# A residual block's second convolution in two goes of 32 output channels, on eight 64x32 tiles of TensorE, with half of the last pass behind the second go

## What is computed

```
x = x + _L0_conv_ref(_gn(x), w1, b1, gamma1, beta1, w2, b2, gamma2, beta2)
...
identity = x
out = conv3x3(x, quantize_weight(w1, W_BITS), b1)
out = jax.nn.relu(batchnorm(out, gamma1, beta1))
out = conv3x3(out, quantize_weight(w2, W_BITS), b2)
out = batchnorm(out, gamma2, beta2)
out = jax.nn.relu(out + identity)
```

## Time and profile before

| | |
|---|---|
| median of 3 runs | 535.56 us (535.4 to 535.96) |
| time of the profiled execution | 536.91 us |
| its span, first to last instruction | 535.1 us |
| busy share of the span | PE 73%, DVE 86%, ACT 62%, POOL 16% |
| first convolution | 14 to 206 us |
| second convolution | 212 to 402 us |
| last pass | 402 to 535 us |

### The profile page before, as it was taken

The page is one execution under the profiler, slowest core; times in us unless marked ns, Lnnn a source line. Parts: engine busy times, 40 slices in busy tenths (PEclk is TensorE's granted clock), DMA queues, the critical chain, the costliest instruction groups (busy, mean ns, idle before and its releaser), DMA issues.

```text
span 535.1 us, 20532 instructions
## 1 busy us (share of the span) xinstructions
PE 392.8 (73%) x9501; PEld 351.2 (66%) x9501; DVE 462.4 (86%) x593; ACT 331.4 (62%) x350; POOL 83.3 (16%) x147
## 2 busy tenths in 40 slices
PE   3999999999999999999999999999991000000000
PEld 1899889999999787899888998888880000000000
DVE  7999989999999757988988887798877999798995
ACT  3898799999999955765555566655515923544200
POOL 2027226666551500000000000000000000000000
PEclk9999999999999999999999999999996555555555
DMA  8934874433333000143333300000066999999997
GB/s 267 358 129 132 269 265 159 181 129 131 129 135 129 8 8 6 46 171 152 129 127 128 124 2 4 4 3 4 2 244 208 355 429 381 431 429 428 432 429 318
DMA packets 21965, 99.21 MB, mean 185 GB/s; under 512 B 6520, under 2 KB 8952, under 8 KB 16504
## 3 DMA queue, kind: packets, MB, share of 16 engines
q1 hardware_dynamic: 20256, 81.55, 40.4%
q10 hardware_dynamic: 1624, 16.36, 7.2%
HBM read 61.48 MB, written 35.50 MB: 181 GB/s over the span
## 4 chain that ended last, share of the span: by engine, by line
PE 72%; DMA 14%; DVE 10%; issue 2%; ACT 1%; SPq 0%; DVEq 0%
PE conv_ps L994 70%; DMA xa<-in_x_dram 11%; DVE slots L948 4%; DVE slots L951 3%; DMA out_dram<-xa 2%; DMA slots<-in_x_dram 1%; DVE xa L951 1%; DVE conv_ps L948 1%; PE conv_ps L957 1%; ACT split L435 0%; DVE gn_tup L674 0%; PE wt_ps L994 0%; PE stat_ps L994 0%; PE conv_ps L992 0%; DVE bn_tup L775 0%
## 5 line engine op out<-in xcount | busy, mean ns | idle before, releaser
L994 PE MATMUL conv_ps<-split,wmat 64*64 64x385 f16 (+3 forms) x9144 | 377.7, 324 | 2.1 <-ACT split L435 1.4
L994 PEld LDWEIGHTS conv_ps<-split,wmat 64*64 64x64 bf16 x9144 | 339.1, 107 | 37.6 <-issue 2.3
L469 ACT ACTIVATE slots<-conv_ps,par,evac_scale 128x784 f32<-128x784 f32 x124 | 123.7, 998 | 95.3 <-PE conv_ps L994 93.4
L775 DVE BATCH_NORM_STATS2 bn_tup<-slots 128x6 f32<-128x392 f32 x166 | 81.9, 555 | 15.6 <-ACT slots L469 15.6
L600 ACT ACTIVATE slots<-slots,skip_b,bn_w 128x3136 f32<-128x3136 f32 (+3 forms) x20 | 45.8, 2340 | 47.6 <-DVE slots L951 29.9
L674 DVE BATCH_NORM_STATS2 gn_tup<-slots 128x6 f32<-128x448 f32 x112 | 61.8, 612 | 0.9 <-DMA slots<-in_x_dram 0.9
L742 DVE TENSOR_TENSOR split<-slots,split 128x3136 f16<-128x3136 f32 (+4 forms) x36 | 57.2, 1607 | 3.5 <-ACT slots L449 0.9
L744 DVE SCALAR_TENSOR_TENSOR split<-slots,split 128x3248 f16<-128x3248 f32 (+3 forms) x18 | 53.6, 2979 | 2.3
L728 DVE TENSOR_SCALAR slots<-slots,bn_w 128x3248 f32<-128x3248 f32 (+3 forms) x18 | 30.4, 1688 | 21.4 <-ACT split L427 20.9
L427 ACT ACTIVATE split<-slots,bn_w 128x3248 f16<-128x3248 f32 x14 | 43.2, 3083 | 0.0
L477 ACT ACTIVATE xa<-conv_ps,par,evac_scale 128x784 bf16<-128x784 f32 x40 | 39.7, 994 | 0.0
(11 more groups left out here) (124 smaller groups left out, 214.4 us busy)
## 6 DMA issues: line engine op xcount, KB each, us to landing
out_dram<-slots SPq DMA_DIRECT2D x13, 1568.0 KB, 15.2
slots<-in_x_dram SPq DMA_DIRECT2D x51, 392.0 KB, 5.6
split<-in_x_dram ACTq DMA_DIRECT2D x5, 1568.0 KB, 23.4
slots<-in_x_dram SPq DMA_DIRECT2D x4, 1568.0 KB, 7.3
y_spill<-slots SPq DMA_DIRECT2D x3, 1624.0 KB, 7.3
slots<-y_spill SPq DMA_DIRECT2D x3, 1624.0 KB, 7.0
y_spill<-slots SPq DMA_DIRECT2D x3, 1568.0 KB, 5.8
slots<-y_spill SPq DMA_DIRECT2D x3, 1568.0 KB, 13.5
```

What stands on the lines that cost most here:

```text
L469: nc.scalar.activation(dst, src, ACT.Identity, bias=bias, scale=scale, accum_out=total).then_inc(evacuated[ph], 1)
L775: ins = nc.vector.bn_stats(bn_tup[:, 2 * (n - first) + s, :], rows[s])
L994: return nc.tensor.matmul(bank[:, r0:r1, w0:w1], lhs, rows[:, top + r0:top + r1, w0 + kx - 1:w1 + kx - 1], start=n == 0 and part is hi_all ...
```

## The change

**Two goes.** The second convolution is done twice over all pairs, first (h = 0) for output channels 0 to 31, then (h = 1) for 32 to 63. The array is cut into eight tiles of K=64, M=32: `a` picks 64 rows, and `b` together with `r` picks 32 columns, where r is one of two rounds that now run together. A pair has two rounds (d = 0, 1) per go instead of four, each of 9 taps x 2 parts x 8 matmuls. Columns per matmul are as before.

**Split parts kept.** In the first go the parts of pair t are written to `KEPT[t]` (two places in `split`, then slots whose contents have been used up), so the second go needs no hi and no lo. For every second pair from pair 3 on (`ACT_MADE2`) ACT, not DVE, also makes the normalised value. The parts of three pairs go to DRAM and come back in the second go.

**First go's values.** They pass through `xa` and are stored to `y2_spill` for 14 pairs (784 KB each).

**Last pass in halves.** An item v is now 32 channels of a pair, [128, 1568]: partition 32*(2b + r) + c holds channel c of image b. Items 0 to 13 (first go's channels) are worked on between the rounds of the second go, items 14 to 31 after it. Each item loads x and stores the result with two DMAs, one per image, and items 2 to 15 first reload their values from `y2_spill`. All of these are issued by SP. There are five pairs of buffers (`NB`). The batchnorm coefficients of the first go come after the second go's first pair.

```diff
+    NR = 2
+    GRAIN = AREA // 2
+    HALF = PIX // 2
...
+    KEPT = [RES, RES + 1, *SOURCE[:NP - 2]]
...
+    NB = len(SUM_BUFFERS)
...
+    ACT_MADE2 = list(range(3, NP, 2))
...
+        def go_views(t, i, h):
+
+            return [t[2 * i + b, 32 * h:32 * h + 32].rearrange("c y w -> c (y w)").rearrange(
+                "c (a r m) -> r c a m", a=2, r=2) for b in range(2)]
+
+        def go_rows(ap):
+
+            return [ap[C * b:C * b + C].rearrange("p (a m) -> p a m", a=2) for b in range(2)]
...
+            def load_input(place, i, h, semaphore):
+                for dst, src in zip(go_rows(granule(place)), go_views(x, i, h)):
+                    sp.dma_start(dst, src).then_inc(semaphore, 16)
...
+            def store_sum(v):
+                h, i, y, _ = sum_item(v)
+                semaphore = sums_stored[v % NB] if v < NP else out_stored
+                for k in range(PARTS[v]):
+                    sp.wait_ge(out_ready, FIRST[v] + k + 1)
+                    for dst, src in zip(go_views(out, i, h), go_rows(y)):
+                        if PARTS[v] == 2:
+                            dst, src = dst[:, :, k], src[:, k]
+                        sp.dma_start(dst, src).then_inc(semaphore, 16)
...
+            sp.wait_ge(lo_ready[1], NR * (NP - 1))
+            load_sum_input(0)
+            load_sum_input(1)
...
+            for v in range(NP):
+                store_sum(v)
...
+                if v + NB < NP:
+                    load_sum_input(v + NB)
+                if v >= 1 and v - 1 + NB < NP:
+                    sum_stored(v - 1)
+                    load_sum_values(v - 1 + NB)
...
+            for t in range(1, NP):
+                evacuate2(NR * t)
+                if t + 2 < NP:
+                    hi2_whole(t + 2)
+                evacuate2(NR * t + 1)
+                if t + 2 in ACT_MADE2:
+                    act2_whole(t + 2)
+            for k in range(NP):
+                evacuate2(NR * (NP + k))
+                if k == 1:
+                    bn_sqrt(1)
+                if k == 2:
+                    sc.wait_ge(bn_coef_ready[1], 1)
+                if k >= 2:
+                    sum_affine(k - 2)
+                evacuate2(NR * (NP + k) + 1)
...
+            for k in range(NP):
+                if k >= 1:
+                    bn_stats2(NR * (NP + k) - 1)
+                if k >= 2:
+                    sums(k - 2)
+                bn_stats2(NR * (NP + k))
+            bn_stats2(2 * NR * NP - 1)
+            bn_coefficients(2)
+            for v in range(NP - 2, 2 * NP):
+                sums(v)
...
+                lhs = wmat[1][C * a:C * a + C, ky * 3 + kx, 32 * h:32 * h + 32]
...
+                        for tap in range(9):
+                            for a in range(2):
+                                for b in range(2):
+                                    for r in range(2):
+                                        mm = eighth(h, tap, part, low, NR * r + d, a, b, n % 3, tap == 8 and low)
+                    mm.then_inc(round_done[1], 1)
```

More of the change, by code:

```diff
@@ L226, in piece, with piece2 @@
+        def piece2(ap, j):
             v = ap.rearrange("p (s r w) -> p s r w", s=2, w=W)
[L227 to L234, removed]
+            return [v[:, :, first:stop].rearrange("p s r w -> p s (r w)") for first, stop in
+                    (((0, RB + 2), (2 * RB, 3 * RB + 2)), ((RB + 2, 2 * RB), (3 * RB + 2, KB)))[j]]
@@ L240, in lo_of, with round_rows @@
             return split[:, t % 2, 1]
[L242 to L251, removed]
+        def round_rows(t, q):
+            return slot_of(t).rearrange("p (s m) -> p s m", s=2)[:, :, W + q * CH:W + (q + 1) * CH]
@@ L350, in _ @@
+            sum_stored(14)
+            load_last_input(13)
+            sum_stored(15)
+            load_last_input(15)
+            sum_stored(10)
+            for v in range(NP, 2 * NP):
+                store_sum(v)
+            sp.wait_ge(out_stored, 32 * (FIRST[2 * NP] - FIRST[NP]))
         @block.gpsimd
@@ L602, in _ @@
+            sum_affine(NP - 2)
+            sum_affine(NP - 1)
+            bn_sqrt(2)
+            sc.wait_ge(bn_coef_ready[2], 1)
+            for v in range(NP, 2 * NP):
+                sum_affine(v)
         @block.vector
@@ L781, in bn_accumulate, with bn_tuples @@
-            def bn_accumulate(ph, first, stop, raw):
-                step = bn_steps[ph]
+            taken = [0, 0, 0]
+            def bn_tuples(z, rows, ins=None):
+                n = taken[z]
+                g = sum(n >= stop for stop in BN_GROUPS[z])
+                first = BN_GROUPS[z][g - 1] if g else 0
+                if n == first and g:
+                    dve.wait_ge(bn_sums[z], g)
+                last = z == 0 and n + 1 == BN_GROUPS[0][-1]
+                for s in range(2):
+                    if last and s == 1:
+                        ins.then_inc(half_seen, 1)
+                        dve.wait_ge(half_taken, 1)
+                    ins = nc.vector.bn_stats(bn_tup[:, 2 * (n - first) + s, :], rows[s])
+                ins.then_inc(bn_seen[z], 1)
+                taken[z] += 1
+                if n + 1 == BN_GROUPS[z][g]:
+                    bn_accumulate(z, first, n + 1, last)
```

849 lines of the change are left out of this document (469 added, 380 removed).

## The result

The changed kernel takes 1444.89 us (median of 4 runs, 1440.6 to 1446.27), the kernel before in the same session 535.76 us (535.4 to 536.28): ratio 2.695, 95% interval 2.689 to 2.702. The predicted 1380 us was 4.5% low, and the mechanism (two engines) was the right one; but the first go was also slower than worked out, and that had a cause that the prediction did not name.

A forecast was written before the change was run, and what follows sets the result against it. It took TensorE to bound the second convolution, DMA and DVE the last pass. Pair 14's lo at 322, plus 1019 for two-engine DMAs, plus 40 for spread transfers gave 1381 us of span, forecast 1380, range 505 to 1450.

The forecast's parts named there:

- What bounds the kernel now: Kernel before: TensorE paces the second convolution, 11.87 us a pair; DMA (94% busy) and DVE the 133 us last pass.
- DMAs, the term that decides: From pair 14's lo on: 128 half-item DMAs with outer count 2 use two engines, 7.96 us each, 1019 us; chance 0.58.
- the 40 for spread transfers: After 322 us: values and parts of three pairs, spread over all sixteen engines, add 40 us.
- First go: First half of the second convolution: a loop of 15.2 us per two pairs, pair 14's lo about 322, TensorE ending at 335.5.
- The sign that I had named: First go: right if two pairs take 15.2 us and TensorE's gaps end on DVE's L926 before odd pairs.
- TensorE: Each go of the second convolution: eight tiles at once take 5.93 us a pair if free, against 11.87 with four.
- Both conditions that I had set: For TensorE's 5.93 us: a matmul and weight load issued every 20 ns, and four column tiles each streaming own data at full rate.
- Range: Whole kernel: 505 to 1450 us, taking in the full-rate case; two engines alone 1310 to 1450.
- Full rate, 515: Half-item DMAs use sixteen engines at full rate, whole kernel 515 us; chance 0.24.
- Half rate, 630: Half-item DMAs use sixteen engines, but 64 of 128 partitions give half the rate, 202 GB/s: 630 us; chance 0.12.
- Four at a time: Second convolution: eight tiles run only four at a time, DMAs being fine: 668 us; chance 0.03.
- 25 ns a matmul: Second convolution: matmul starts never closer than about 25 ns, a go 117 us, DMAs being fine: 533 us; chance 0.03.

The follow-up runs named there:

- the forms measured alone: No block computed, only loads of x in differing forms: 64 runs of 3136 bytes took 32.2 us with outer count 2 ([2][32]), 16.8 with 4, 7.8 with 64.
- the first experiment: Changed kernel with each half-item DMA cut along its outer count of 2 into two DMAs of 32 partitions: 654.12 us, ratio 1.222 to the kernel before.
- the small-DMA run: The 654.12 us kernel with cut half-item DMAs, each now moving only 98 of the 784 floats of a row: 608.14 us (one run).

## Why the prediction was right, and where it was not

**What bounds the kernel now**: its condition, "provided that the DMAs keep their pace", is what broke. Nothing to correct in the reading of before.

**DMAs, the term that decides**: right. The doubt that was left (outer count or number of runs) is settled by q10's 202 packets and by the forms measured alone. Price of one DMA: 7.96 us predicted; [2][32] alone took 32.18 / 8 = 4.02 us for half of the bytes, 8.04. In the kernel: from the first half-item load, at 357.98, to the end 1086 us; less the 40 for spread transfers, which is still the estimate of the prediction, 8.17 us each. 1059 us were predicted: +27.

**First go**: the step that failed. The loop was given as 15.2 us for two pairs, with rounds of 2.97. The start of lo of pairs 9 and 11 (DVE), what stands ahead of the second (ACT), TensorE's waits from 212 to 340 us, and the first half-item loads (SP), in the changed kernel:

```profile
302.44 3.54 DVE L926 TENSOR_TENSOR slots<-slots 128x3248 f16<-128x3248 f32 x1 [3.31 <-ACT slots L586]
...
322.38 3.54 DVE L926 TENSOR_TENSOR slots<-slots 128x3248 f16<-128x3248 f32 x1 [6.04 <-ACT slots L586]
```

```profile
309.46 1.00 ACT L621 ACTIVATE xa<-conv_ps,par,evac_scale 128x784 f32<-128x784 f32 x1 [0.68 <-PE conv_ps L1217]
312.50 1.00 ACT L621 ACTIVATE xa<-conv_ps,par,evac_scale 128x784 f32<-128x784 f32 x1 [2.03 <-PE conv_ps L1217]
313.40 3.08 ACT L575 ACTIVATE slots<-slots,bn_w 128x3248 f16<-128x3248 f32 x1
318.26 1.00 ACT L621 ACTIVATE xa<-conv_ps,par,evac_scale 128x784 f32<-128x784 f32 x1 [1.77 <-PE conv_ps L1217]
319.16 3.08 ACT L586 ACTIVATE slots<-slots,bn_w 128x3248 f32<-128x3248 f32 x1
```

```profile
PE conv_ps L1217 <- issue: 33.9, 20, 4.6
```

```profile
357.98 19.39 SPq L365 DMA_DIRECT2D split<-in_x_dram  x4
```

19.9 us here; the six loops from pair 3 to pair 15 took 17.0 to 24.1 us, 19.5 on average. Between lo's end (305.98) and the PSUM move at 318.26 TensorE ends the round under way and does pair 9's two, and each of the three moves waits for it. So its rounds have become longer than ACT's own work between them, and they set the loop, where I had let only the first count. The sign that I had named did not come: TensorE's gaps end on nothing ("issue"), none on L926. With 9 us lost up to lo of pair 3 (247.3, not 238.3) and 4.3 in each loop, lo of pair 14 is done at 354.2 and not 322. The first half-item load goes out another 4 us later, at 358, since it stands behind the store of pair 13's values, whose PSUM move ends at 357.6: +36 in all. With the +27 above that is the whole miss, 1444 against 1381 of span.

The trace also shows part of why these rounds are longer than 3.7 us per 128 matmuls would make them. From 262 us to the end of the go the packets of the instruction queue start 3.3 to 4.3 us apart, but 4.9 to 5.2 us five times, each time while one pair's values (784 KB) are being stored, and before 262 us, with the spilled pairs on their way, up to 7.9. After two of these gaps the clock was lower for a while: after the idle 1.99 us from 302.23 and 2.53 us from 322.58 the granted clock was 0.69 and 0.75 for 4 us, where it had been 1.00.

**TensorE**: "5.93 us a pair and go" is what failed. Both conditions that I had set hold: issue can be as fast as 10 ns, and four column streams run at full rate within a piece. There was a third that I had not thought of: instructions must arrive. It was 9.4 us a pair (151 / 16) with the DMA engines busy at 0.43, and 11.5 (184 / 16) at 0.79. In the second go the price did not show in the total, since the DMAs hid it; it shows in the +36 of the first go and in the 118 us of the first experiment.

**Range.** The 1450 at its end came from a slower rate of the engines (1430) and held nothing for a longer first go. That 1444.89 lies inside it by 5 us, with 36 us from the first go in it, is in part luck.

**The rivals.** *Full rate, 515*, which had a chance of 0.24: excluded. Even with the transfers of the last pass nearly gone it is 608: predicted first go 123, second 95, rest 85; measured 160, 151, 84. Only the last was right. *Half rate, 630*: close to the 654 of the repaired kernel, but in part by luck, since TensorE's supply has its share in that time and the last pass moved 271 GB/s, not 202. *Four at a time* and *25 ns a matmul*: neither is how it works. Within a piece matmuls start 20 ns apart. The 25 ns of the Trainium skill, "TensorE: Matmul & The Clock Gate", section "Wait — 56ns, not 53.3ns?", does not hold there, though the mean of 28 ns comes out above it.

The whole: 909 us slower = 791 for two engines + 118. Of the 118, 46 depend on the bytes of the half-item DMAs (in supply and transfers). The other 72 are two goes that cost 19.4 us a pair (160 + 151 us) instead of 11.87, 121 us more, less the 49 us of the last pass that now lie beside the second go (84 us against 133). With the best supply seen (3.6 us per 128 matmuls, and 300 matmuls a pair and go: 8.4 us) it would be 212 + 2 x 134 + 84 = 564 us. By this estimate from these runs no repair of the DMAs makes this scheme faster than 535.6.

Left open: why pairs of 64-partition DMAs gain next to nothing in loads alone, though they go to both halves; and the share of the clock in the longer goes (0.88 granted in the first experiment's second go against 0.95 in the small-DMA run). It fell behind gaps of TensorE in the two places above, so it is partly a consequence.

## What to carry to other kernels

Write down the outermost count on both sides of each DMA before you regroup data; a count of 2 in front of 64 rows made a transfer four times as long as sixteen engines need for the same 64 rows (32.2 against 7.8 us) and cost more than the whole kernel, and 62 is no better than 2. Count TensorE's instructions as well as its columns: in these runs, below about 28 ns per matmul and weight load the supply sets the pace, so splitting tiles or rows to smaller ones stops paying there, and pays less still beside heavy DMA traffic. The signs are pieces of 128 matmuls with gaps that end on nothing ("issue"), and an instruction queue whose packets come as often as the pieces.

## What the runs showed of the hardware that was not expected

Instructions reach TensorE in packets of 16,384 bytes, 128 matmuls with their weight loads. One comes every 3.3 to 4.0 us at best, about 6 beside loads over 128 partitions, up to 10 beside 64-partition ones, and as often as at rest beside loads on two engines. Four 64x64 tiles of 392 columns use one in 5.3 us (47.9 us for 1152), which leaves room: in its second convolution the kernel before had no gap in 100 us. The Trainium skill, "Runtime: NRT & Kernel Launch", section "Instruction fetch mechanics", tells of such blocks of 256 instructions, and says that their fetch is hidden by a floor of the issue; here it is not, 3.7 us against the 2.5 that 128 matmuls at 20 ns take.

DMAs over 64 partitions moved more in a mix of loads and stores (317 GB/s) than in loads alone (213).
